# Softplus as one ScalarE function, and the softmax's exponentials placed ahead of a burst of decays

## What is computed

```python
x = x + 0.5 * _L0_ffn_ref(_layernorm(x), w_router, w_gating, w_gate, w_up, w_down)
x = x + _L0_attn_ref(_layernorm(x), W_in, conv_w, conv_b, W_x, W_dt, b_dt, A_log, D_param, W_out)
x = x + 0.5 * _L0_ffn_ref(_layernorm(x), w_router, w_gating, w_gate, w_up, w_down)
```

```python
router_probs = softmax(x @ w_router)
gate_weights = softmax((x @ w_gating) / 0.1)
h = silu(g) * u                      # g = x @ w_gate[e], u = x @ w_up[e]
cw = router_probs * gate_weights
cw = cw / (sum(cw) + 1e-09)
out = sum over e of (h @ w_down[e]) * cw[e]
```

```python
dt = softplus(dbl[..., :64] @ W_dt + b_dt)
dA = exp(dt[..., None] * A)                    # the "decays", 16 states
dBx = (dt * xc)[..., None] * Bm[:, :, None, :]
h = dA_t * h + dBx_t;  y = sum over n of h * C_t
```

## Time and profile before

| | us |
|---|---|
| median of 3 runs | 1244.83 (1244.51 to 1245.08) |
| span of the profiled execution | 1243.0 |
| PE busy | 1237.4 (100%) |
| PEld busy | 1066.6 (86%) |
| DVE busy | 1143.1 (92%) |
| ACT busy | 1004.7 (81%) |
| POOL busy | 450.6 (36%) |

### The profile page before, as it was taken

The page is one execution under the profiler, slowest core; times in us unless marked ns, Lnnn a source line. Parts: engine busy times, 40 slices in busy tenths (PEclk is TensorE's granted clock), DMA queues, the critical chain, the costliest instruction groups (busy, mean ns, idle before and its releaser), DMA issues.

```text
span 1243.0 us, 20366 instructions
## 1 busy us (share of the span) xinstructions
PE 1237.4 (100%) x7212; PEld 1066.6 (86%) x7212; DVE 1143.1 (92%) x1353; ACT 1004.7 (81%) x2022; POOL 450.6 (36%) x574
## 2 busy tenths in 40 slices
PE   9999999999999999999999999999999999999999
PEld 7888888888888888888888888888888888888887
DVE  5958799999998999999999999998999999998877
ACT  7678888988887989887988989898888987865554
POOL 0021144335462443543534425344453344531000
PEclk9999999999999999999999999999999999999999
DMA  8312488798877879878889787977778779881222
GB/s 232 97 30 44 86 176 176 154 184 171 168 159 155 173 150 196 168 165 165 171 175 184 162 179 149 190 163 154 153 165 175 163 155 194 169 179 35 61 52 59
DMA packets 118135, 184.59 MB, mean 148 GB/s; under 512 B 11280, under 2 KB 34448, under 8 KB 118032
## 3 DMA queue, kind: packets, MB, share of 16 engines
q0 software_dynamic: 54384, 99.11, 45.7%
q1 hardware_dynamic: 63648, 84.16, 25.3%
HBM read 81.46 MB, written 2.69 MB: 68 GB/s over the span
## 4 chain that ended last, share of the span: by engine, by line
PE 90%; ACT 3%; DVE 3%; DMA 2%; issue 2%; POOL 0%; DVEq 0%; ACTq 0%; POOLq 0%
PE PS L1070 27%; PE PS L961 18%; PE PS L964 18%; PE PS L962 18%; PE PS L1066 2%; PE PS L1062 1%; PE PS L1064 1%; PE PS L1128 1%; DMA XT<-YE 1%; DVE HB L1310 1%; PE PS L1113 1%; DMA Y<-HS 1%; PE PS L997 1%; DVE HS L1408 1%; ACT HB L1521 1%
## 5 line engine op out<-in xcount | busy, mean ns | idle before, releaser
L1070 PEld LDWEIGHTS PS<-WD,HB 128*128 128x128 f32 x3424 | 422.3, 191 | 23.7 <-issue 1.5
L1070 PE MATMUL PS<-WD,HB 128*128 128x128 f32 x3424 | 424.5, 275 | 0.0
L1310 DVE TENSOR_TENSOR HB<-PS,HB 128x1024 f32<-128x1024 f32 (+1 forms) x336 | 322.6, 961 | 77.2 <-PE PS L964 56.1
L1521 ACT ACTIVATE HB<-PS 128x512 f32<-128x512 f32 x512 | 293.6, 596 | 101.7 <-PE PS L964 99.6
L1712 POOL DMA_DIRECT2D Y<-HS x252 | 220.8, 957 | 343.8 <-DVE HS L1416 164.0
L961 PE MATMUL PS<-XH,WG 128*128 128x512 f32 x509 | 221.3, 435 | 0.0
L961 PE MATMUL PS<-XH,WU 128*128 128x512 f32 x512 | 205.3, 401 | 0.7 <-DVE HB L1310 0.5
L964 PE MATMUL PS<-XH,WU 128*128 128x512 f32 x512 | 201.2, 393 | 0.0
L964 PE MATMUL PS<-XH,WG 128*128 128x512 f32 x509 | 200.8, 395 | 0.0
L962 PE MATMUL PS<-XH,WU 128*128 128x512 f32 x512 | 200.5, 392 | 0.0
L962 PE MATMUL PS<-XH,WG 128*128 128x512 f32 x509 | 199.2, 391 | 0.0
(11 more groups left out here) (168 smaller groups left out, 1466.1 us busy)
## 6 DMA issues: line engine op xcount, KB each, us to landing
BCB<-BCD SPq DMA_DIRECT2D x128, 512.0 KB, 5.2
Y<-HS POOLq DMA_DIRECT2D x252, 256.0 KB, 6.0
XT<-YE POOLq DMA_DIRECT2D x106, 256.0 KB, 5.0
YE<-CWD SPq DMA_DIRECT2D x20, 256.0 KB, 4.5
AT<-YE POOLq DMA_DIRECT2D x14, 256.0 KB, 3.3
WD<-in_L_ffn_w_down_dram SPq DMA_DIRECT2D x8, 256.0 KB, 6.2
XT<-in_L_attn_x_dram SPq DMA_DIRECT2D x7, 256.0 KB, 6.5
out_dram<-XT SPq DMA_DIRECT2D x7, 256.0 KB, 5.7
```

Source lines behind the costliest of these rows:

```text
L1070: z = pe.matmul(part(g, j), HB[:, i % NH, j * P:(j + 1) * P], WD[:, e, c, :], start=c == 0 and j == 0, stop=c == FC - 1 and j == SUB - 1)
L1310: v.tensor_tensor(H, PS[:, NG + i % 2:NG + i % 2 + n, :], H, ALU.mult).then_inc(S["v_h"], 1)
L1521: a.activation(HB[:, i % NH, :], gate(i), ACT.Silu).then_inc(S["a_sil"], 1)
```

## The change

Softplus becomes one activation function. `b_dt` only copies the product with its bias out of PSUM (Identity, into DX), and `b_soft` runs Softplus from DX into XS. The addition is gone on both paths (`ADDED`, `b_add`, L1378), and the decays wait for `a_soft` alone. The costs in the plan follow. `b_soft` now also carries the wait for the convolution (`v_cv`), since XS is first written there.

The exponentials of a softmax are no longer placed where they come up. `prep` puts the position on a list (`wanted`) and waits until `decays()` places a burst, and `decays()` then puts `p_exp` directly ahead of the burst, at a planned cost of 0.45 us. The wait ends after `PATIENCE = 25` us of planned time, or at once while no decay has been placed yet or all have been.

```diff
-ADDED = (1, 2, 3)
-SUMMED = 10.0
+PATIENCE = 25.0
...
-        at = step("p_exp", p, after=at, a=3.0)
+        wanted.append((p, at))
+        limit = clock["pe"] + PATIENCE
+        while p not in exp_at and decayed[0] and decayed[0] < NT * NS and clock["pe"] < limit:
+            yield False
+        if p not in exp_at:
+            wanted.clear()
+            exp_at[p] = step("p_exp", p, after=at, a=3.0)
+        at = exp_at[p]
         at = step("p_norm", p, after=at, p=2.4)
...
-            at = step("b_dt", t, j, bk, pe=.47, a=1.1)
-            give(bk[0], "a_relu", 2 * t + j + 1, at + MARGIN)
+            at = step("b_dt", t, j, bk, pe=.47, a=.55)
+            give(bk[0], "a_pre", 2 * t + j + 1, at + MARGIN)
...
-        at = step("b_soft", t, after=at, a=4.5)
+        dt_at[t] = at = step("b_soft", t, after=at, a=3.6)
         yield True
-        if t in ADDED:
-            yield from until(at)
-            at = step("b_add", t, after=at, p=.9) + SUMMED
         yield from until_v(at + LATEST)
-        at = step("b_dx", t, after=at, v=1.2 if t in ADDED else 2.4)
-        dt_at[t] = at - 1.2
+        at = step("b_dx", t, after=at, v=1.2)
...
                 dt_at[m // NS] < clock["pe"] + .5 and clock["a"] < clock["pe"] + CALM)):
+            if wanted and wanted[0][1] < clock["a"] + .2:
+                p, _ = wanted.pop()
+                exp_at[p] = step("p_exp", p, a=.45)
             at = step("s_da", m, after=dt_at[m // NS], a=2.56 + 1.24 * BURST)
...
-                        v.tensor_tensor(dt, dt, dx, ALU.add).then_inc(S["v_dt"], 1)
...
-                    a.activation(DX[:, t % 2, j, 0:T], bank(b), ACT.Abs, bias=bdt_t[:, j:j + 1]).then_inc(S["a_abs"], 1)
-                    a.activation(XS[:, t % 2, j, 3:3 + T], bank(b), ACT.Relu, bias=bdt_t[:, j:j + 1]).then_inc(S["a_relu"], 1)
+                    a.activation(DX[:, t % 2, j, 0:T], bank(b), ACT.Identity, bias=bdt_t[:, j:j + 1]).then_inc(S["a_pre"], 1)
...
-                    a.preload_act_table_set("natural_log_exp_and_others")
-                    a.activation(dx, dx, ACT.Exp, scale=-1.0).then_inc(S["a_sexp"], 1)
-                    wt.wait_ge(S["a_sexp"], t + 1)
-                    a.activation(dx, dx, ACT.Ln, bias=1.0).then_inc(S["a_soft"], 1)
+                    wt.wait_ge(S["v_cv"], 6 * t + 6)
+                    a.activation(XS[:, t % 2, :, 3:3 + T], DX[:, t % 2, :, 0:T], ACT.Softplus).then_inc(S["a_soft"], 1)
...
-                elif k == "b_add":
-                    t = s[1]
-                    wt.wait_ge(S["a_soft"], t + 1)
-                    wt.wait_ge(S["a_relu"], 2 * t + 2)
-                    gp.dma_start(XS[:, t % 2, :, 3:3 + T], DX[:, t % 2, :, 0:T], accum_op=ALU.add).then_inc(S["c_dt"], 16)
```

More of the change, by code:

```diff
@@ L321, in timetable @@
     haste, inputs = set(), {0}
+    wanted, exp_at = [], {}
     stored, begun_y, put = set(), set(), {-2, -1}
@@ L706, in macaron_program @@
         S = {}
-        for n in ("c_small c_con c_wr c_acc c_y0 c_y1 c_bcd c_dt o_x init w_hi w_lo dv "
+        for n in ("c_small c_con c_wr c_acc c_y0 c_y1 c_bcd o_x init w_hi w_lo dv "
                   "m_ct m_at a_ct a_hh v_hh a_wd v_wh v_hl v_wd v_ts v_at c_ct c_cw0 c_cw1 c_cw2 m_g m_u m_dn m_tr m_lg m_win m_wx m_wt m_wo m_end v_end "
-                  "a_ye a_sil a_sum a_mean a_sq a_xn a_car a_lr a_xh a_exp a_neg a_rmh a_win a_tap a_yc a_dbl a_abs a_relu a_sexp a_soft a_yd a_da "
-                  "v_h v_mx v_norm v_cw v_ye v_mset v_rm v_halo v_cv v_bc v_db v_sc v_hc v_yz v_x2 v_dt v_dx v_y v_wr v_lt v_xl v_ve v_nm v_xn "
+                  "a_ye a_sil a_sum a_mean a_sq a_xn a_car a_lr a_xh a_exp a_neg a_rmh a_win a_tap a_yc a_dbl a_pre a_soft a_yd a_da "
+                  "v_h v_mx v_norm v_cw v_ye v_mset v_rm v_halo v_cv v_bc v_db v_sc v_hc v_yz v_x2 v_dx v_y v_wr v_lt v_xl v_ve v_nm v_xn "
                   "c_x0b m_tr0 v_mv a_sd v_x0 v_xh p_ve s_rs p_nm p_sub p_sm pl").split():
@@ L1370, in _ @@
                     t = s[1]
-                    dt, dx = XS[:, t % 2, :, 3:3 + T], DX[:, t % 2, :, 0:T]
                     wt.wait_ge(S["a_yc"], 2 * t + 2)
-                    if t in ADDED:
-                        wt.wait_ge(S["c_dt"], 16 * (ADDED.index(t) + 1))
-                    else:
-                        wt.wait_ge(S["a_soft"], t + 1)
-                        wt.wait_ge(S["a_relu"], 2 * t + 2)
-                        v.tensor_tensor(dt, dt, dx, ALU.add).then_inc(S["v_dt"], 1)
-                        wt.wait_ge(S["v_dt"], t + 1 - sum(k < t for k in ADDED))
-                    v.tensor_tensor(dx, dt, Y[:, t % 2, :, :], ALU.mult).then_inc(S["v_dx"], 1)
+                    wt.wait_ge(S["a_soft"], t + 1)
+                    v.tensor_tensor(DX[:, t % 2, :, 0:T], XS[:, t % 2, :, 3:3 + T], Y[:, t % 2, :, :], ALU.mult
+                                    ).then_inc(S["v_dx"], 1)
                 elif k == "b_dtl":
@@ L1585, in _ @@
                     wt.wait_ge(S["m_wt"], 2 * t + j + 1)
-                    wt.wait_ge(S["v_cv"], 6 * t + 6)
                     if t >= 2:
                         wt.wait_ge(S["v_db"], (t - 1) * NS)
-                    a.activation(DX[:, t % 2, j, 0:T], bank(b), ACT.Abs, bias=bdt_t[:, j:j + 1]).then_inc(S["a_abs"], 1)
-                    a.activation(XS[:, t % 2, j, 3:3 + T], bank(b), ACT.Relu, bias=bdt_t[:, j:j + 1]).then_inc(S["a_relu"], 1)
+                    a.activation(DX[:, t % 2, j, 0:T], bank(b), ACT.Identity, bias=bdt_t[:, j:j + 1]).then_inc(S["a_pre"], 1)
                 elif k == "b_soft":
                     t = s[1]
-                    dx = DX[:, t % 2, :, 0:T]
-                    wt.wait_ge(S["a_abs"], 2 * t + 2)
-                    a.preload_act_table_set("natural_log_exp_and_others")
-                    a.activation(dx, dx, ACT.Exp, scale=-1.0).then_inc(S["a_sexp"], 1)
-                    wt.wait_ge(S["a_sexp"], t + 1)
-                    a.activation(dx, dx, ACT.Ln, bias=1.0).then_inc(S["a_soft"], 1)
+                    wt.wait_ge(S["a_pre"], 2 * t + 2)
+                    wt.wait_ge(S["v_cv"], 6 * t + 6)
+                    a.activation(XS[:, t % 2, :, 3:3 + T], DX[:, t % 2, :, 0:T], ACT.Softplus).then_inc(S["a_soft"], 1)
                 elif k == "b_y":
```

## The result

| | before | after |
|---|---|---|
| median, us | 1244.68 | 1261.12 (1260.23 to 1265.64) |
| ratio | | 1.0135, 95% interval 1.0118 to 1.0153 |
| span of the profiled execution | 1243.0 | 1263.8 |

The change makes the kernel slower, by 16.4 us in the median. The forecast was 1242.9, its range ended at 1246.8. The execution that was profiled is the slowest of four, 4.5 us above the median. The kernel before was run again beside every kernel of this study, so its median differs a little from one comparison to the next (1244.6 to 1244.8).

What follows compares the result with a forecast made beforehand. PE was taken as the bound, with 4.7 us of gaps as the whole budget. Terms of -1.8, -0.3 and +0.2 summed to -1.9 us, so 1244.8 becomes 1242.9 us, range 1240.3 to 1246.8.

Steps and rivals of the forecast that it cites:

- What bounds the kernel: PE is the bound, busy 958.5 of 960 us from 160 to 1120 us, with 22 gaps adding to 4.7 us.
- the bound on the gain: With all 22 PE gaps gone, the median of 1244.8 becomes 1240.1; no saving on ACT or DVE brings more.
- The costs on ScalarE: Softplus, Relu and table-load savings on ACT: 50.5 us busy and 15 us of waiting, busy time falling to about 954 us.
- The PSUM bank and softplus on PE: Shared bank returned one activation sooner, 0.6 to 0.7 us for each of 16 products; 1.1 us priced directly on PE.
- the faster case of the forecast: All or most PE gaps go, since ACT and DVE get air: 1240.1 to 1242.3 us, chance 0.34.
- by itself this brings nothing, because PE has expert work all the time and waits for no scan: Tiles 1 to 3 start decays some 11 us sooner without the addition; counted as 0, bounds -1 and +2 us.
- what of it reaches PE: Share of the 4.7 us of PE gaps removed, plus a new wait: -1.8 - 0.3 + 0.2 = -1.9 us.
- Since the plan is made anew, I give it two thirds: Of 2.7 us of PE gaps at or behind softplus, `b_dt` or softmax, two thirds go: 1.8 us.
- nothing reaches PE: Rival: scans start sooner, DVE is denser, new gaps of the same size appear: 1244.0 to 1247.3 us, chance 0.16.
- The new wait at the reciprocal: DVE reaches the reciprocal 2.55 us sooner relative to ACT; 0.7 us at each of 12, 8 us, PE sees 0.2.
- The one sign that I had named: PE's waits for L1310, the product of gate and up, fall from 6.7 us in the weight load to about 4.
- this rival: DVE waits 1.9 us at each of 12 reciprocals, PE pays a third of 23 us: 1250.2 us, chance 0.10.

Runs made afterwards that it cites:

- The planned end of the exponentials: Changed kernel with position 4's layernorm kept ahead of tile 2's, plus moved exponentials' planned end 2.55 us later: 1247.83 us, against 1249.85 without that.
- the planned softplus kernel with the layernorms in order: Changed kernel without the moved exponentials, planned anew, with a condition keeping position 4's layernorm ahead of tile 2's: 1244.60 us, ratio 0.9998.
- the run with the cost of 4.6: Kernel before with only the planned cost of b_soft raised from 4.5 to 4.6 us, planned anew: 1247.19 us, ratio 1.0020.
- the first experiment: Kernel before, order of steps kept, only softplus exchanged: Identity and one Softplus for Abs, Relu, Exp, Ln and the addition: 1241.81 us, ratio 0.9977.

## Why the prediction was wrong

**What bounds the kernel** was read rightly, and the bound on the gain held: no kernel of this study has a median under 1241.8, with 1240.1 as the floor that I gave.

**The costs on ScalarE** held as single prices: Softplus 1.06 us, eight loads each way, 12 loads fewer at the bursts, the wait for L1656 gone where the softmax moved. The sum of ACT's busy time didn't (974 us, not 954). 13.6 us of the 20 went back into weighings that the plan gave it; I treated the plan's decisions as constant. Some 4.5 us more were never there to save: in the old order, with the same loads, ACT is 15.2 us less busy and not 19.7. The times of single instructions overlap (four decays of 712 ns take 2.56 us together), so a sum of single times is more than the busy time that goes with them.

**The PSUM bank and softplus on PE** held in sign, and were sized too low. I gave them 1.2 us, alone; on the old order they bring 3.0, as the weight load's waits for gate and up fall too. In the old order the first part is the faster case of the forecast.

**The step that failed** is the sentence "by itself this brings nothing, because PE has expert work all the time and waits for no scan", and with it the whole of "what of it reaches PE". It took the stalls of one plan as the stock from which the change can only take. In fact position 4 needs tile 0's Mamba output with little to spare: in the kernel before, XH is complete at 300.0 and the position's first product starts at 307.0. In the changed kernel XH is complete at 316.8. I saw that position 4 was thin for its softmax, and didn't ask the same of its input. One layernorm of tile 2 ahead of it uses up the 7 us of slack and more: 5.0 us of idle, 1.2 us of idle in two pieces behind it, and the slow clock. It costs 9.2 to 11.3 us of the 16.4 by the runs that take it away.

**"Since the plan is made anew, I give it two thirds"** had the wrong sign. A new plan costs 2.6 us in the run in which one planned cost moves by 0.1. That the plan of before is a good one with few gaps, and most others are worse, is likely from this and was not sampled further. I had noticed that everything is planned anew and made no rival of it; *nothing reaches PE*, with its end at 1247.3, was the nearest one, and it left out that an order could be lost.

**The new wait at the reciprocal** was there, and its sum was right: 7.8 us in the changed kernel, where I had 8. It comes in 8 pieces and not in 12 of 0.7 us, and with bounds of 0 and 23 us the close hit is in part luck. What PE pays for it I had at 0.2 us, since DVE's waits of today don't show on PE. In the old order with the exponentials moved on ScalarE alone, PE pays 30.5 us for 29.6 us of VectorE's waiting, in pieces of up to 4.8 us. In the changed kernel, whose pieces are 1.6 us at most, the price isn't measured: the one run that bears on it, 2.0 us for 3.3, isn't clear of noise. The one sign that I had named and that speaks to it went the wrong way: the weight load's waits for the product of gate and up grew from 6.7 us to 8.7, and PE itself waits another 4.0. So the mechanism of this rival exists, and with a third, or 0.2 us in the forecast's own sum, I priced it too low for the long waits.

**The sum of the loss.** The changed kernel stands 19.3 us over the same Softplus in the old order, 1241.8. The order of two layernorms is 11.3 of it (with what else that new plan moved). The planned end of the exponentials is 2.0, within noise. The new plan by itself is 2.8, from 1241.8 to the 1244.6 of the planned softplus kernel with the layernorms in order; the run with the cost of 4.6 gives 2.6 for the same thing. The last 3.2 us, from there to 1247.8, come with the moved exponentials and the plan that goes with them. The one large gap in that kernel is the one at 748 us, 2.5 us by the pitch, behind the load of B and C; the kernel at 1244.6 has no gap over 0.6 from 160 to 1120 us. So at most a small part of the 3.2 us is left for the 4.8 us that VectorE still waits at the reciprocal. Whether the moved exponentials or only the new plan made that load late stays open.

**A version that beats both** is the first experiment's: Softplus in the order planned for five operations, 1241.8 us.

## What to carry to other kernels

When a planner writes the order, a change of a cost is a change of the whole order: price the change first on the old order, and then compare the two lists for pairs that have changed places. Look for the step that begins a stage from another stage's output, and write its precedence into the plan rather than leave it to a race. An engine at 97% that isn't the bound has little room to wait: in an order that was kept, 29.6 us more of its waiting were 30.5 us more of time, while 27.5 us of work taken off an engine at 80% were worth nothing.

## What the runs showed of the hardware

TensorE's granted clock was 1.00 throughout the kernel before. After the idle stretch of 5.0 us it came back at the lower of its two levels, 1.2 GHz in place of 2.4, as the mean of 0.83 from 305 to 325 us and the pitch of 0.43 us show, and stayed there to about 320 us. In the kernel before with the swapped layernorms it was still 1.00 behind the wait of 1.1 us at 308.9, and 0.57 from 313 to 321 us, behind the wait of 3.5 us. In the kernel with the exponentials moved on ScalarE alone it fell behind PE's idle of 3.6 us at 329.3 (0.60 from 328 to 332), of 2.75 at 625.3 (0.50 from 626 to 629) and of 2.8 at 708.0, and not behind 2.6 at 948.0 (1.00). It didn't fall behind the 2.3 us of idle at 748 us either. A long stall costs more than its length: ten matmuls at 0.43 us and not 0.23 are 2 us more here.

That is in line with what the Trainium skill says ("TensorE: Matmul & The Clock Gate", Part 1: The HAM clock gate), that an engine left idle falls back to the lower clock.

At a table load, in the kernel before, in the changed one and in the first experiment's, ScalarE's next activation starts 0.01 us behind the load unless it waits for an input: merged or not, a switch is 1.28 us. The drain of 1380 ns that the Trainium skill ("ScalarE: Activation LUTs", What ACT_TABLE_LOAD costs) adds to a load doesn't show in these traces.
